# First MLP pass: the second half of its hidden columns takes the token blocks in reverse order, and the second pass follows that order

## The reference

```python
xn = _layernorm(x, g2, be2)
xm = xn * (1.0 + sc_m[:, None, :]) + sh_m[:, None, :]
h = jax.nn.gelu(xm @ W1 + b1, approximate=False)
x = x + gt_m[:, None, :] * (h @ W2 + b2)
```

## Time and profile before

| what | value |
|---|---|
| median of three runs | 2127.44 us (2126.57 to 2131.51) |
| the profiled execution, its own time | 2128.58 us |
| its span, first to last instruction | 2126.8 us |
| mean granted TensorE clock | 0.999 |
| busy: PE, DVE, ACT, POOL | 98%, 69%, 48%, 50% of the span |
| first MLP pass | about 1454 to 1775 us |
| second MLP pass | about 1775 to 2127 us |

### The profile page before, as it was taken

The page is one execution under the profiler, slowest core; times in us unless marked ns, Lnnn a source line. Parts: engine busy times, 40 slices in busy tenths (PEclk is TensorE's granted clock), DMA queues, the critical chain, the costliest instruction groups (busy, mean ns, idle before and its releaser), DMA issues.

```text
span 2126.8 us, 31156 instructions
## 1 busy us (share of the span) xinstructions
PE 2086.1 (98%) x11134; PEld 1392.8 (65%) x11134; DVE 1477.0 (69%) x3114; ACT 1010.5 (48%) x1884; POOL 1068.9 (50%) x473
## 2 busy tenths in 40 slices
PE   8999999999999999999999999999998999999999
PEld 7888885444444444444454444688886888888887
DVE  5877877777777777777777765567867875444433
ACT  2111115566566665666666666566744554222221
POOL 2001006989879797997979974688125310000000
PEclk9999999999999999999999999999999999999999
DMA  7548348136252352614336231596465446444442
GB/s 282 193 159 267 134 159 199 37 81 141 67 125 54 89 111 68 143 47 109 77 72 146 56 91 42 164 364 237 165 205 172 164 171 215 137 135 158 154 139 94
DMA packets 177122, 298.82 MB, mean 141 GB/s; under 512 B 13374, under 2 KB 39046, under 8 KB 176776
## 3 DMA queue, kind: packets, MB, share of 16 engines
q1 hardware_dynamic: 156376, 255.94, 41.8%
q10 hardware_dynamic: 20592, 40.90, 5.1%
HBM read 187.20 MB, written 109.58 MB: 140 GB/s over the span
## 4 chain that ended last, share of the span: by engine, by line
PE 74%; POOL 11%; DVE 6%; issue 4%; DMA 3%; ACT 2%; SPq 0%; POOLq 0%; DVEq 0%; ACTq 0%; PEldq 0%
PE acc L862 12%; PE st L1454 9%; POOL psum_k L1209 9%; PE mx L1434 9%; PE o_ps L1471 9%; PE p_acc L2443 8%; PE p_acc L2425 7%; PE m_free L2443 4%; PE p_tp L2443 4%; PE m_free L2425 4%; PE r_ps L1478 2%; DVE part L1314 2%; DMA x_scratch<-k_whole 1%; DMA x_scratch<-x 1%; PE r_ps L1492 1%
## 5 line engine op out<-in xcount | busy, mean ns | idle before, releaser
L1253 ACT ACTIVATE prob<-st 128x512 f32<-128x512 f32 (+3 forms) x1280 | 609.2, 540 | 374.1 <-PE st L1454 359.3
L1209 POOL TENSOR_TENSOR psum_k<-psum_k,prob 128x2048 f32<-128x2048 f32 (+1 forms) x150 | 663.7, 4425 | 20.7 <-ACT prob L1253 5.8
L1314 DVE TENSOR_REDUCE part<-mx 128x1 f32<-128x512 f32 x707 | 458.1, 685 | 74.9 <-PE mx L1434 70.5
L1454 PE MATMUL st<-q_st,k_st 98*128 98x512 f32 (+3 forms) x1280 | 490.9, 395 | 4.0 <-PE r_ps L1478 1.4
L1434 PE MATMUL mx<-k_st,qx_st 96*128 96x512 f32 (+3 forms) x1196 | 442.8, 395 | 10.1 <-DVE part L1314 3.3
L1454 PEld LDWEIGHTS st<-q_st,k_st 98*128 98x128 f32 x1280 | 241.4, 189 | 267.2 <-ACT prob L1253 152.5
L1310 DVE CUSTOM_DVE_ANT_0 unused<-mx,mask_row 128x512 bf16<-128x512 f32 (+2 forms) x489 | 229.0, 486 | 118.8 <-PE mx L1434 108.9
L1434 PEld LDWEIGHTS mx<-k_st,qx_st 96*128 96x128 f32 x1196 | 223.5, 189 | 129.9 <-DVE part L1314 60.7
L1471 PE MATMUL o_ps<-prob,v_sb 128*32 128x512 f32 (+3 forms) x2560 | 297.4, 539 | 3.5 <-POOL prob L1192 3.5
L1209 POOL TENSOR_TENSOR psum_k<-prob 128x2048 f32<-128x2048 f32 x23 | 105.4, 4581 | 205.7 <-ACT prob L1253 205.4
L2290 DVE TENSOR_TENSOR m_g_lo<-m_g_raw,m_g_hi 128x512 fp32r<-128x512 f32 x128 | 86.8, 691 | 170.9 <-ACT m_g_hi L2108 170.8
(11 more groups left out here) (269 smaller groups left out, 3533.8 us busy)
## 6 DMA issues: line engine op xcount, KB each, us to landing
m_g_raw<-g_scratch SPq DMA_DIRECT2D x128, 256.0 KB, 2.7
k_st<-qk_scratch SPq DMA_DIRECT2D x96, 256.0 KB, 8.2
qx_st<-qk_scratch SPq DMA_DIRECT2D x96, 256.0 KB, 5.0
q_st<-qk_scratch SPq DMA_DIRECT2D x96, 256.0 KB
qk_scratch<-st_hi ACTq DMA_DIRECT2D x16, 1024.0 KB, 4.2
qk_scratch<-st_lo ACTq DMA_DIRECT2D x16, 1024.0 KB, 7.0
g_scratch<-g_beside SPq DMA_DIRECT2D x64, 256.0 KB, 2.3
over_k_whole<-xm_scratch SPq DMA_DIRECT2D x28, 512.0 KB, 6.7
```

What stands on the lines that cost most here:

```text
L1209: nc.gpsimd.tensor_tensor(dst, src, prob[:, s % BUF, :, m:], ALU.add).then_inc(pool_added, 1)
L1253: nc.scalar.activation(prob[:, s % BUF, h, m:], st[n % RING][:, m:], ACT.Exp, scale=SCALE).then_inc(exp_done, 1)
L1314: nc.vector.tensor_reduce(most, bank[:, 0:w], AX.X, ALU.max).then_inc(mx_free, 1)
L1454: nc.tensor.matmul(st[n % RING][:, m:], k_st[u][0:MROWS, h, kt * P:(kt + 1) * P], q_st[0:MROWS, pos % 2, h, m:], start=True, stop=True).th ...
```

## The change

The second half of the first pass (cycles 16 to 31, sets 4 to 7) takes the blocks in the order 3, 2, 1, 0. Block 3 is in the buffer already when cycle 16 begins, so there are seven versions and six changes; version 3 lasts for eight cycles. Order.version, begins and tokens hold the new numbering, and what was written at q % HALF now asks where a version begins. The split of set 4 moves from the end of cycle 14 to the head of cycle 15, by an entry in WEIGHTS_AT, as sets 5 to 7 have it. The second pass takes the chunks in the order 6, 7, 4, 5, 2, 3, 0, 1 (CHUNKS), with the matching rows of g, x2, output, gate and bias.

```diff
     def version(self, q):
-        return q // HALF
+        return q // HALF - (q >= HALF * SUPER)
+    def begins(self, v):
+        return HALF * (v + (v >= SUPER))
+    def tokens(self, v):
+        return v if v < SUPER else 2 * (SUPER - 1) - v
...
-        NV = NQ // HALF
+        NV = NQ // HALF - 1
+        CHUNKS = [2 * v + u for v in reversed(range(SUPER)) for u in range(2)]
...
-        WEIGHTS_AT = {1: 2, 2: 3, 16: 5, 17: 6, 18: 7}
+        WEIGHTS_AT = {1: 2, 2: 3, 15: 4, 16: 5, 17: 6, 18: 7}
...
             def load_raw(v):
-                first = 2 * (v % SUPER)
+                first = 2 * R.tokens(v)
...
-                if q % HALF == 0 and 2 <= q // HALF + 1 < NV:
-                    load_raw(q // HALF + 1)
+                v = R.version(q) + 1
+                if 2 <= v < NV and q == R.begins(v) - HALF:
+                    load_raw(v)
...
-                if 0 < v < NV - 1 and rank == 1:
-                    token_sums(v + 1, 0)
-                    token_sums(v + 1, 1)
+                if 2 <= v < NV and q == R.begins(v) - 3:
+                    token_sums(v, 0)
+                    token_sums(v, 1)
...
-                if q == HALF * SUPER - 2:
-                    weight_high(HALF)
...
-                if q == HALF * SUPER - 2:
-                    weight_low(HALF)
...
-                sp.dma_start(ring_raw[i % GB][:, 0, :], K.g[j * P:(j + 1) * P, cols(n)]).then_inc(g_loaded[i % GB], 16)
+                sp.dma_start(ring_raw[i % GB][:, 0, :], K.g[j * P:(j + 1) * P, cols(CHUNKS[n])]).then_inc(g_loaded[i % GB], 16)
```

More of the change, by code:

```diff
@@ L1865, in store_g @@
                 sp.wait_ge(activated, R.activated[it, q])
-                tile, n = 2 * R.weights(q) + row - 1, 2 * (R.version(q) % SUPER) + col - 1
+                tile, n = 2 * R.weights(q) + row - 1, 2 * R.tokens(R.version(q)) + col - 1
                 sp.dma_start(K.g[tile * P:(tile + 1) * P, cols(n)], hid[it][q % 2][:, :]).then_inc(stored[it][q % 2], 16)
@@ L1880, in load_g @@
                     sp.wait_ge(used, (HT - 1) * ((i - GB) // HT) + (i - GB) % HT + 1)
-                sp.dma_start(ring_raw[i % GB][:, 0, :], K.g[j * P:(j + 1) * P, cols(n)]).then_inc(g_loaded[i % GB], 16)
+                sp.dma_start(ring_raw[i % GB][:, 0, :], K.g[j * P:(j + 1) * P, cols(CHUNKS[n])]).then_inc(g_loaded[i % GB], 16)
             def load_x2(n):
-                sp.dma_start(ms[n % 2][:, :, :], K.x2[cols(n), :].rearrange("(t p) d -> p t d", p=P)).then_inc(m_loaded, 16)
+                sp.dma_start(ms[n % 2][:, :, :], K.x2[cols(CHUNKS[n]), :].rearrange("(t p) d -> p t d", p=P)).then_inc(m_loaded, 16)
             sp.wait_ge(x2_ready, TT)
@@ L1948, in sync @@
                     sp.wait_ge(out_ready, TT * n)
-                    sp.dma_start(out[cols(n - 1), :].rearrange("(t p) d -> p t d", p=P), ms[(n - 1) % 2][:, :, :]).then_inc(out_stored, 16)
+                    sp.dma_start(out[cols(CHUNKS[n - 1]), :].rearrange("(t p) d -> p t d", p=P), ms[(n - 1) % 2][:, :, :]).then_inc(out_stored, 16)
                 if j == 14 and n < NCH - 1:
@@ L1957, in sync @@
                 sp.wait_ge(out_ready, TT * n + s + 1)
-                sp.dma_start(out[n * CH + s * P:n * CH + (s + 1) * P, :], ms[n % 2][:, s, :]).then_inc(out_stored, 16)
+                sp.dma_start(out[cols(CHUNKS[n]), :][s * P:(s + 1) * P, :], ms[n % 2][:, s, :]).then_inc(out_stored, 16)
             sp.wait_ge(out_stored, 16 * (n + TT))
@@ L2019, in gpsimd @@
             for q in range(NQ):
-                v, rank = q // HALF, q % HALF
+                v = R.version(q) + 1
                 if q in (2, 3):
                     token_sums(1, q - 2)
-                if 0 < v < NV - 1 and rank == 1:
-                    token_sums(v + 1, 0)
-                    token_sums(v + 1, 1)
+                if 2 <= v < NV and q == R.begins(v) - 3:
+                    token_sums(v, 0)
+                    token_sums(v, 1)
                 if 13 <= q < 13 + HALF:
@@ L2063, in x_high @@
                 if v:
-                    act.wait_ge(product_done, R.done(k, HALF * v - 1))
+                    act.wait_ge(product_done, R.done(k, R.begins(v) - 1))
                 if k in T_ORDER:
@@ L2330, in add_bias @@
                 dve.wait_ge(m_loaded, 16 * (n + 1))
-                link(nc.vector.tensor_tensor(ms[n % 2][:, s, :], gbias[:, batch(n), :], ms[n % 2][:, s, :], ALU.add))
+                link(nc.vector.tensor_tensor(ms[n % 2][:, s, :], gbias[:, batch(CHUNKS[n]), :], ms[n % 2][:, s, :], ALU.add))
             def finish(n):
@@ L2338, in finish @@
                         dve.wait_ge(out_ready, TT * n + s - 1)
-                    nc.vector.tensor_tensor(gated[:, s % 2, :], totals[n % 2][s][:, :], K.gate[:, 1, batch(n), :], ALU.mult).then_inc(sum_free, 1)
+                    nc.vector.tensor_tensor(gated[:, s % 2, :], totals[n % 2][s][:, :], K.gate[:, 1, batch(CHUNKS[n]), :], ALU.mult).then_inc(sum_free, 1)
                     dve.wait_ge(sum_free, TT * n + s + 1)
@@ L2418, in product @@
                     pe.wait_ge(w_split, 2 * (R.weights(q) + 1))
-                if q % HALF == 0:
+                if q == R.begins(R.version(q)):
                     pe.wait_ge(x_split, len(PRODUCTS) * R.version(q) + X_AT[k] + 1)
```

## The result

The changed kernel takes 2117.48 us (median of six runs, 2116.66 to 2118.52) against 2128.28 us for the kernel before in the same series (2126.54 to 2131.51): a ratio of 0.9947, with a 95% interval of 0.9937 to 0.9956, faster by 0.5%. The forecast was 2116.6 us, the range 2115.2 to 2119.9. The profiled span went from 2126.8 to 2115.2 us.

What follows compares the result with a forecast made beforehand. TensorE was taken to bound both passes, losing time in cycles 15 to 17 and 20. Gains 5.67 + 3.49 + 0.82 + 0.89 = 10.87 us from a median of 2127.44 gave 2116.6 us, range 2115.2 to 2119.9.

Steps and rivals of the forecast that it cites:

- the first part: Cycles 15 to 17: removing the block change brings them to 9.52 us, saving 5.67, 3.49 and 0.82, together 9.98 us.
- The third part: Block change at cycles 19 to 20: its load leaves SP sooner, so cycle 20 falls from 10.41 to 9.52, saving 0.89 us.
- begins to cost at 1606.2: Head of cycle 15: set 4's sums coming after 1606.2 would cost a microsecond for each microsecond late.
- the other bound of 1600.5: Set 4's POOL sums, four of 0.75 us after its load landed at 1597.46, are ready at 1600.5 at the latest.
- (a): Cycle 20's block change stays dear because w_lo of set 7 slows POOL: gain 9.98 us, 2117.5; chance 0.22.
- the third term: Cycle 20's saving of 0.89 us: all if POOL ends before DVE's splits, nothing if one t_sum overlaps each.
- (b): Cycles 16 and 17 stay late for the weight sets themselves: gain 5.67 us, 2121.8; chance 0.05.
- (c): Second pass gives back the first's gain, for instance by late g tiles: no change, 2127.4; chance 0.03.
- (d): Set 4 still unsummed at the head of cycle 15, ACT and DVE stop: slower, 2133.8; chance 0.02.

Runs made afterwards that it cites:

- the run with the held load: Changed kernel with SP holding back the load of block 2 (for cycle 20) until product 5 of cycle 17 is done; 2118.16 us, ratio 0.9951.
- eight extra subtractions: Changed kernel with eight extra POOL subtractions, results not used, ahead of set 4's sums, without block load; 2118.76 us, ratio 0.9953.
- sixteen: Changed kernel with sixteen extra POOL subtractions, about 20 us, results not used, ahead of set 4's sums; 2126.82 us, ratio 0.9990.
- the swap on POOL: Kernel before, with POOL making set 4's four sums ahead of the block's eight differences; old block order and split place; 2125.81 us, ratio 0.9987.
- both moves: Kernel before, old block order, with POOL's set 4 sums ahead of the differences and set 4's split at the head of cycle 15; 2125.71 us, ratio 0.9986.

## Why the prediction was right, and where its story was not

**The sum.** The three terms of the first part were 5.67, 3.49 and 0.82 us, and the profile has cycles 15, 16 and 17 at exactly the 9.52 that was taken from cycle 18. That step was sound because it did not rest on the cause: cycle 18 had all the work that would stay, and TensorE lost nothing to it. The third part, 0.89 us at cycle 20, came in full too. Beyond the sum, which had not counted it, cycle 24 gave 0.23 us, probably the same knock-on as in the run with the held load: in the kernel before the load left SP at 1673.73, 24.4 us before cycle 24 as it did there. Its row in the kernel before:

```profile
1698.18:1707.93 9.75, 9.75 (x43) 7.80 (x42) 1.00 0.28 108
```

That is 11.1 us in the first pass; with a few hundredths of cycles 0, 6, 21 and 25 the trace has 11.2, and of the 11.6 us of span the other 0.4 or so lie ahead of the first pass, in its start (0.46 earlier), which varies more than that between executions. The forecast lay 0.9 us low because the kernel before, measured again, was at 2128.28 and not 2127.44.

**The due time.** The bound "begins to cost at 1606.2", 4.6 us into cycle 15, was a little early. With eight extra subtractions the sums came 1.4 us into cycle 15 (1604.36 − 1602.91) and cost nothing; with sixteen 12.2 us into it (1612.72 − 1600.48), 7.6 past the bound, and TensorE stopped for 6.28 us. Set 4 itself came at 1592.66, well under the other bound of 1600.5.

**The story.** The step that failed is in the account of the cause: "Then ACT and DVE, already late, have the seven splits of the token block to do as well, so cycles 16 and 17 are late too". It makes the lateness of set 4 the condition for the loss of these two cycles. With the weights on time and nothing waiting for POOL (the differences left out) they still took 12.17 and 10.35 us, against 13.01 and 10.34 in the kernel before. What the runs show in its place is that a block change that meets new weights costs even when nothing is late, some 2.3 us by the estimate above, and that making the weights punctual puts POOL's differences beside DVE's splits, so that 7.62 of 9.98 us stayed. The first half of the account stands: the 5.67 us of cycle 15, the pause and the half clock behind it, are gone from that cycle when set 4 is on time. How the 4.31 us of cycles 16 and 17 in the kernel before divide between the lateness and the load is not shown.

The block change is at its place in the kernel before the only one that falls into cycles in which new weight sets are summed and split: at cycle 12 the same change is free, and at cycle 16 with POOL's sums and DVE's weight splits taken away it costs 1.66 us. The chain of waits in the earlier trace rows was read rightly as to what came last in cycle 15; it could not show what would come last next. The sum was safe from this, since the change takes away both; my forecast for a cheaper edit, the swap on POOL, was 0 to 3 us of loss, and 7.50 were measured.

**The rivals.** (a) was out: t_sum's pair beside w_lo of set 7 did slow down, to 4.16 us, but the load had left SP at 1621.02, 18.2 us before cycle 19 and not 16.8, so the differences ended at 1641.66, before the first split at 1642.81. The Trainium skill (SBUF — State Buffer, Who interferes with whom) says that a VectorE instruction with two SBUF inputs and a GpSimd instruction that reads SBUF shut each other out. The runs agree with it as to the size: two w_lo grew together by 4.27 − 2.09 = 2.18 us, which is less than two whole differences (2 x 1.28 = 2.56). All or nothing, as I had put it for the third term, it was not: nearly the same stretched splits (1.93 and 2.31 us in the kernel before, 1.75 and 2.31 with the held load) cost 0.89 us at cycle 20 in the one kernel and 0.38 in the other. (b), (c) and (d) did not happen, and (c) was far off: even the natural order of the second pass cost nothing. The rows that (c) was judged by, show busy times and not waits; the list of TensorE's waits in the second pass is empty in both kernels.

## What to carry to other kernels

When a periodic job (here a change of token block every four cycles) falls into a stretch with another one (new weights), look at each engine's load over that stretch, and move one of the two out. Making one of them punctual gave back only a quarter here, because it pushed the other's work to a place where it slowed DVE. The chain of waits names what came last this time; to know what a smaller edit would bring, take the named cause away on the chip and see what is late next. For a larger edit the safer number is the time of a like stretch elsewhere in the same trace that has exactly the work that will remain.

## What the runs showed of the hardware

- POOL and DVE slowed each other where DVE took both operands from SBUF: in the kernel with both moves DVE's split of a weight set went from 2.09 to 4.27 us and POOL's pair of differences from 2.55 to 4.49 us. DVE's sums of products, which take one operand from PSUM, stayed at 0.67 to 0.69 us beside the same POOL work.
- A stop of TensorE did not always bring the half clock. With both moves a pause of 2.31 us in cycle 16, with 0.75 and 1.02 us some microseconds behind it, left the granted clock at 1.00. With the swap alone pauses of 0.52 and 2.46 us, with 1.6 us of matmuls between them, were followed by a stretch at half clock (0.89 over cycle 16). After the 6.28 us with sixteen subtractions the stretch reached into the next cycle (0.87 and 0.90).
